# A later second weight load, one subtraction moved and two fill products fewer, in the opening of a two-layer expert kernel

## What is computed

```python
x = x + xattn(layernorm(x), token_ids, ctx, ctx, ctx)    # 4 experts, picked by token id
x = x + ffn(layernorm(x), router_w, wg, wu, wd)          # 8 experts, picked by argmax of x @ router_w.T

# first layer, expert e, one 512x512 matrix C = ctx[e] used three times:
y = (silu(h @ C.T) * (h @ C.T)) @ C.T
# second layer: weights cut to -1/0/1 by the mean of their absolute values,
# activations rounded to 8 bits by the largest of their row:
s = 1 / clip(mean(abs(w)), 1e-5);  wq = clip(round(w * s), -1, 1) / s
y = bitlinear(square(relu(bitlinear(x, wg[e]))) * bitlinear(x, wu[e]), wd[e])
```

## Time and profile before

| | us |
|---|---|
| median of three runs | 255.06 |
| the profiled execution | 255.76 |
| its span (first to last instruction) | 253.8 |
| PE busy in the span | 234.7 (92%) |
| DVE busy | 218.2 (86%) |
| ACT busy | 210.5 (83%) |
| POOL busy | 164.2 (65%) |

### The profile page before, as it was taken

How to read it: one execution, slowest core, us unless ns; L and a number is a source line. 1 busy time by engine, 2 the same in 40 slices (tenths; PEclk the granted TensorE clock), 3 DMA queues, 4 the chain that set the end, 5 groups by cost and what they waited for, 6 DMA issues and landing times.

```text
span 253.8 us, 5722 instructions
## 1 busy us (share of the span) xinstructions
PE 234.7 (92%) x1409; PEld 172.4 (68%) x1419; DVE 218.2 (86%) x675; ACT 210.5 (83%) x324; POOL 164.2 (65%) x325
## 2 busy tenths in 40 slices
PE   2398999999999999999999999999999999999990
PEld 2255778888888888888888888886455555555530
DVE  5879989899889988799888988879999999999871
ACT  2767899799888988898888888787899999999960
POOL 4362665868778777588777664347538786757653
PEclk9999999999999999999999999999999999999996
DMA  5999944935754499784566534541388962211110
GB/s 203 425 359 362 424 180 151 362 131 226 243 210 146 134 354 406 283 324 157 201 249 227 147 127 169 207 146 69 98 237 250 310 251 85 83 41 68 70 37 0
DMA packets 13726, 51.71 MB, mean 204 GB/s; under 512 B 2750, under 2 KB 2750, under 8 KB 10112
## 3 DMA queue, kind: packets, MB, share of 16 engines
q1 hardware_dynamic: 8816, 37.91, 42.4%
q0 software_dynamic: 4880, 13.44, 14.4%
HBM read 40.49 MB, written 13.48 MB: 213 GB/s over the span
## 4 chain that ended last, share of the span: by engine, by line
PE 73%; DVE 10%; DMA 9%; issue 4%; ACT 1%; POOL 1%; SPq 0%; DVEq 0%; ACTq 0%
PE bank L1555 33%; PE bank L1677 19%; PE bank L1539 9%; PE bank L1647 5%; DMA staged<-weight_chunks 4%; PE bank L1669 4%; DMA ternary<-weight_chunks 3%; PE bank L1784 2%; DMA staged<-x_rows 1%; DVE ternary L957 1%; DVE ctx_lo L1000 1%; PE bank L1574 1%; POOL out_rows L643 1%; DVE ternary L1019 1%; DMA token_ids<-token_ids_in 1%
## 5 line engine op out<-in xcount | busy, mean ns | idle before, releaser
L1677 PE MATMUL bank<-ternary,qT 128*128 x179 | 43.6, 380 | 0.5
L694 ACT ACTIVATE ternary<-staged 128x2048 bf16<-128x2048 f32 x20 | 38.0, 1899 | 2.5 <-DMA staged<-weight_chunks 2.5
L700 ACT ACTIVATE ternary<-staged,w_scale 128x1536 int16<-128x1536 f32 x20 | 31.4, 1576 | 2.3 <-DVE w_scale L1014 0.6
L1677 PEld LDWEIGHTS bank<-ternary,qT 128*128 128x128 bf16 x184 | 17.7, 97 | 20.2 <-issue 5.4
L562 POOL DMA_INDIRECT x_rows<-row,store_at x19 | 25.5, 1340 | 6.8 <-POOL store_at L554 5.0
L643 POOL DMA_INDIRECT out_rows<-late_rows,late_token x18 | 19.0, 1057 | 9.4 <-DVE late_rows L1350 8.0
L473 POOL DMA_INDIRECT x<-x_rows,gather x16 | 18.5, 1155 | 10.2 <-DVE gather L969 6.3
L1677 PE MATMUL bank<-ternary,rT 128*128 x87 | 22.6, 380 | 0.4 <-ACT rT L812 0.2
L747 ACT ACTIVATE p<-bank,rstd 128x512 f32<-128x512 f32 x19 | 13.0, 684 | 11.6 <-PE bank L1555 11.5
L1555 PE MATMUL bank<-ctx_hi,pT_hi 128*128 x76 | 22.3, 415 | 0.1
L1555 PE MATMUL bank<-ctx_hi,hT_hi 128*128 x76 | 22.3, 414 | 0.0
(11 more groups left out here) (237 smaller groups left out, 658.6 us busy)
## 6 DMA issues: line engine op xcount, KB each, us to landing
staged<-weight_chunks SPq DMA_DIRECT2D x20, 1024.0 KB, 5.5
late_rows<-x_rows SPq DMA_DIRECT2D x18, 260.0 KB, 3.7
ternary<-ctx_chunks SPq DMA_DIRECT2D x4, 1024.0 KB, 8.3
ternary<-weight_chunks SPq DMA_DIRECT2D x4, 1024.0 KB, 9.8
x_rows<-filler SPq DMA_DIRECT2D x1, 2080.0 KB, 12.9
staged<-x_rows SPq DMA_DIRECT2D x5, 260.0 KB, 2.7
x_rows<-row,store_at POOLq DMA_INDIRECT x19, 6.0
out_rows<-late_rows,late_token POOLq DMA_INDIRECT x18
```

The source lines that it names most:

```text
L694: nc.scalar.activation(ternary[:, m * K * D:(m + 1) * K * D], staged_of(i), ACT.Abs, accum_out=abs_sum[:, 2 * i:2 * i + 1]).then_inc(abs_r ...
L700: nc.scalar.activation(ternary[:, m * K * D + DVE_COLS:(m + 1) * K * D].bitcast(I16), staged_of(i)[:, DVE_COLS:], ACT.Copy, scale=w_scale[ ...
L1677: last = pe.matmul(ps[:, :], left[:, k * P:(k + 1) * P], ternary[:, bass.ds(e * (3 * K * D) + (kind * K + k) * D, D)], start=(k == 0), sto ...
```

## The change

SP waits for `gathering` to reach 1 before it issues w1. DVE runs the first half of context 0's low halves ahead of `mean_of(0)` and `scale_of(0)` in place of behind them. The fills behind `sum_mean(0)` go from nine to seven; the three behind `sum_mean(1)` stay.

```diff
-WARM_UP = (9, 3)
+WARM_UP = (7, 3)
...
             load_context(0)
             load_weights(0)
             load_context(1)
+
+            sp.wait_ge(gathering, 1)
             load_weights(1)
-
             sp.wait_ge(gathering, 2)
             load_context(2)
             load_weights(2)
...
             dve.wait_ge(gathering, 1)
+            low_half(0, 0)
             mean_of(0)
             scale_of(0)
-            low_half(0, 0)
             moments_of(0)
             aggregate(0)
             normalise(0)
```

## The result

| | before | after |
|---|---|---|
| median, us | 255.34 (4 runs, 254.93 to 255.88) | 259.11 (4 runs, 258.43 to 259.94) |
| ratio of after to before | | 1.0148, 95% interval 1.0103 to 1.0193 |
| the profiled execution, us | 255.76 | 258.43 |
| its span, us | 253.8 | 256.5 |

The kernel is slower by 1.5%, 3.8 us by the medians. Repeated later beside 29 runs of before the ratio was 1.0113 (1.0073 to 1.0153).

What follows compares the result with a forecast made beforehand. PE was taken to bound the kernel, so an opening delay reaches the end. Compute path +2.4 us, load path +1.9 beside it, other parts 0: 257.5 us against the 255.06 median, range 256.3 to 260.0.

Steps and rivals of the forecast that it cites:

- rival A: Clock not held: after PE's idle gap, fills and first product run at 1.2 GHz; 2.0 us more, 259.5 us, chance 0.22.
- w1's landing: Opening, load of w1: issued at about 11.66 us, lands at 17.2, 3.1 us later than before, against 1.5 us of slack.
- Its effect on the eviction: ACT, block 0: `evict_hT(0)` waits behind w1's sum and starts at 19.2 us instead of 17.60, +1.6.
- The first product's start: PE, block 0: first product starts at 20.85 us instead of 18.34, +2.5, behind `sum_mean(1)` and three fills.
- the sign that I had set for it: First product on PE: its twelve matmuls taking 5 us would show that the clock was not held.
- The load path: Loads behind w1: the queue runs 1.9 us later, so w4 lands at about 35.2 us instead of 33.28.
- The reckoning by holes in the queue: DMA queue around w1: delay between 1.2 us, the difference of the holes, and 2.5 us, w1's own transfer; 1.9 taken.
- the compute path decides: At w4's sum: ACT arrives at about 35.6 us, after w4 has landed, so the compute path's +2.4 us counts.
- Parts 2 and 3: Opening: moved subtraction on DVE and two fewer fills on PE; each gains 0, though transposes could start 0.86 us sooner.
- The gather's gain: Gather 0 without w1 beside it: DVE waits 0.7 us less, `h` about 0.8 us sooner, worth nothing because ACT is busy.
- the steps behind 27.7 us would pass the shift on: Layer one from 27.73 us: PE-bound block steps of 8.0 us add the opening's delay to the end almost one for one.

Runs made afterwards that it cites:

- the new order: Kernel after with block 0's eviction ahead of `sum_abs(1)` on ACT and matching re-orderings on DVE and PE; 1.0015 of before.
- the runs of each part alone: Kernel before with only seven fills in place of nine, 1.0017; kernel before with only the first low-halves subtraction moved ahead of `mean_of(0)`, 0.999.
- the wait alone: Kernel before with only SP's wait for `gathering` 1 ahead of w1, nine fills and no moved subtraction; 1.008.
- ctx2 sooner: Kernel before, w1 issued at once, with ctx2 issued behind the first gather in place of the second; 1.0084.
- early fills: Kernel before with three more fills at 10.6 us, where PE waits for the tables; 1.0008.
- the attempt with ctx2 sooner and seven fills: Kernel before with ctx2 behind the first gather, eviction ahead of `sum_abs(1)` with matching orders, three fills at 10.4 us, seven behind `sum_mean(0)`; 1.0093.

## Why the prediction was right, and where its terms were off

The forecast was slower by 2.4 us, 257.5 us, in 256.3 to 260.0. The measured 259.11 us lies inside, towards the top, where the forecast met rival A. By the medians that is a loss of 3.8 us, 2.8 in the repeat and 2.7 by the profiles, against 2.4; the profile explains its own 2.7, and the 1.1 us that the first medians show beyond it stays unexplained.

**w1's landing.** Right in kind, a little too late: taken as 17.2, it was 16.69 (11.64 + 5.05 on the chain). It lay near the lower bound of 4.8 us; ctx2's 7.7 us was not the neighbour to weigh. Its effect on the eviction came out at +1.01, not +1.6.

**The first product's start.** Forecast +2.5, measured +1.12. This is the step that was mis-sized. Half a microsecond is w1, and 0.1 the sum, which with its read kept ACT 1.9 us and not 2.0. The other 0.8 is PE's part. I had it start beside the eviction, rightly, but then laid `sum_mean(1)` (0.57), the three fills (0.81) and 0.15 end to end, so that the fills "now stand between `sum_mean(1)` and `first_product(0)`" in the open, 1.65 us from the eviction's start to the product's. It took 0.85. The records on PE overlap: `sum_mean(1)` began at 18.76 and lasted 0.38, the fills began at 19.00 already, and the product at 19.46, while the fills' record runs to 19.81. The eviction ran from 18.61 to 19.19, so the product began 0.27 us behind it, where before it was 0.14 (18.20 to 18.34): `sum_mean(1)` and the fills cost 0.13 us at most beyond the eviction. The rows of before show the same overlap, 17.56 + 0.81 against a product from 18.34.

**The clock, rival A.** Given 0.22, it happened in both profiles of the kernel after, and by the sign that I had set for it: twelve matmuls in 4.7 us. I priced it at 2.0 us; the product took 1.7 us more, and holding the clock gave 1.2 us back at the end. The way was partly another one: the clock had reached its upper level (three fills in 0.81 us) and then fell in the product, behind a gap of 2.1 us. The row that I lacked was one with a gap of that length at the upper level. The Trainium skill's statement ("TensorE: Matmul & The Clock Gate", section "What's actually happening") that the throttled clock is the default and activity releases it fits these traces: with eight fills in the gap, 0.50 became 1.00. I should have put the gap and the clock together as one mechanism in place of two rivals, since the forecast itself said that PE would stand for 2.4 us.

The two errors nearly cancelled: +1.12 and +1.7 make 2.8, against a forecast of 2.4 without the clock. That the number came so near is luck in part; that the late w1 reaches the first product through ACT's order, and costs more than 1 us there, is not.

**The load path.** I had w4 1.9 us late at 35.2. In the kernel after it was issued at 23.08 and took 9.6 us, so it landed at 32.7, 0.6 us sooner than before. The reckoning by holes in the queue was wrong there. In the new order w4's sum began at 33.99, 0.7 us later than before, but 33.89 with w1 early and seven fills; so the runs show no delay of the load path that is clear of its scatter. That the compute path decides in the kernel after held: ACT reached w4's sum at 35.84, 2.5 us later than before (2.4 forecast), with no wait for the load.

**Parts 2 and 3, and the gather.** Priced at nothing, and the runs of each part alone agree within their intervals (1.0017, 0.999). The gather's gain was 0.84 us against my 0.7 of waiting and 0.8 for `h`, and it was lost where I said, before ACT's sum. For the two fills there is a hint of a cost together with the late load: after has 1.0113 to 1.0148 and the wait alone 1.008, but the intervals overlap, the two weren't run side by side, and their profiles have the same span, 256.5 us. This stays open.

**After the opening.** That the steps behind 27.7 us would pass the shift on held: 210.7 us from the extra load to the end before, 210.9 after.

## What to carry to other kernels

Before a load is put off, find the first instruction that needs it and then what is queued behind that instruction on the same engine: here block 0's eviction, and PE's mean ahead of the first product, made block 0 wait for a load that it doesn't use. When the engine that a delay leaves idle is TensorE, price the clock with it, and fill the gap if it can't be closed. A gain on one of two paths that run level stops at the other: take the second one's slack from the trace first.

## What the runs showed that I had not expected

A gap of TensorE of 2.1 to 2.3 us was followed by a granted clock of 0.50 for about 3 us (the kernel after twice, the wait alone, ctx2 sooner). The fall came just as work resumed (the wait alone, whose fills then ran at 0.48 us each) or about 1 us later (the other three, whose first matmuls behind the gap ran at the upper level). With a gap of 3.7 us it came inside the gap and lasted 6 us and more. In the kernels without such a gap (before, the new order, early fills) it read 1.00 through the opening. It isn't the whole truth, though: in the attempt with ctx2 sooner and seven fills it read 1.00 throughout while four transposes took 1.11 us, three fills 1.49 and the first four matmuls 1.98, the pace of 1.2 GHz:

```profile
20.07 1.98 PE L1559 MATMUL bank<-ctx_hi,hT_hi 128*128 x4
```

```profile
20.00:21.00 1.00, 1.00 (x4) 0.82 (x3) 1.00 (x2) 1.00 (x1) 1.00 (x1) 1.00 1.13 467
```

I read this as a clock that hadn't risen yet, since its seven fills ahead of the gap took 0.45 us each too; the granted clock in the record shows a fall, and not that the first rise is still to come. The time of equal matmuls is what to read.

A gather of 256 KB depends strongly on what the load queue holds when it is handed over: 3.7 to 3.9 us to landing with no load left in flight and w1 issued 0.15 us behind it, 4.5 with one 1 MB load in flight, 7.1 (6.3 in the second such kernel) with one in flight and another issued 0.15 us behind it. That ctx2 waits for `gathering` 2 and not only 1, which the change left alone, is worth 0.8% of the kernel.
